# A graph layer's edge tiles cut from 128 edges to 127

## The reference, cut to what matters

```python
def _rgcn_layer(x, W, root, bias, src, dst, seg):
    agg = segment_sum(x[src], seg, num_segments=N_REL * N_NODES)
    agg = agg.reshape(N_REL, N_NODES, -1)
    return einsum('rnd,rde->ne', agg, W) + x @ root + bias
...
h = relu(layer(relu(layer(xn, 0)), 1));  h = sigmoid(layer(h, 2))
x = x + h + mix(xn)          # mix: linear attention over all nodes and a feed-forward part
x = x + moe(layernorm(x))    # 8 experts, the top 2 of each node
```

## Time and profile before

| | |
|---|---|
| median of three runs without the profiler | 8040.71 us (8016.86 to 8065.2) |
| span of the profiled execution, first to last instruction | 6522.0 us |
| median less the span | 1518.7 us |
| busy in the span | PE 83%, POOL 71%, PEld 62%, DVE 31%, ACT 16% |
| phase 0, then the gathers of layers 1, 2 and 3 | 0 to 389, 389 to 2404, 2424 to 4450, 4471 to 6489 us |
| mean granted TensorE clock | 0.920 |

### The profile page before, as it was taken

How to read it: one execution, slowest core, us unless ns; L and a number is a source line. 1 busy time by engine, 2 the same in 40 slices (tenths; PEclk the granted TensorE clock), 3 DMA queues, 4 the chain that set the end, 5 groups by cost and what they waited for, 6 DMA issues and landing times.

```text
span 6522.0 us, 82564 instructions
## 1 busy us (share of the span) xinstructions
PE 5410.7 (83%) x22990; PEld 4060.0 (62%) x22990; DVE 2019.4 (31%) x5385; ACT 1061.6 (16%) x2756; POOL 4625.3 (71%) x4909
## 2 busy tenths in 40 slices
PE   8977777777777778888888888887888888888888
PEld 4445555555555546666666666666777777777776
DVE  3321211122222223332333333333444444444444
ACT  2211111111111111111111111111222222222222
POOL 1057777777777767777777777776777777777776
PEclk9989898889898889999999999999999999999999
DMA  6654444444444444544554444444433333433333
GB/s 195 180 155 137 137 137 137 137 137 137 137 137 137 137 143 144 147 146 146 147 148 146 146 145 146 147 146 149 116 115 115 115 115 115 115 115 115 116 115 93
DMA packets 354380, 887.88 MB, mean 136 GB/s; under 512 B 86234, under 2 KB 179294, under 8 KB 335623
## 3 DMA queue, kind: packets, MB, share of 16 engines
q0 software_dynamic: 232080, 633.91, 33.0%
q10 hardware_dynamic: 114178, 243.16, 12.8%
q1 hardware_dynamic: 7740, 5.99, 0.3%
HBM read 697.11 MB, written 185.60 MB: 135 GB/s over the span
## 4 chain that ended last, share of the span: by engine, by line
POOL 44%; PE 30%; issue 15%; ACTq 5%; DMA 3%; ACT 1%; POOLq 1%; DVE 0%; DVEq 0%; SPq 0%
POOL ring L501 44%; PE ps_out L1403 11%; PE ps_y L1371 8%; PE ps_tr L1570 2%; PE ps_b L1558 2%; DMA ring<-table,gather_idx 2%; PE ps_c L1371 1%; PE ps_b L1371 1%; PE ps_c L1558 1%; ACTq L619 1%; ACTq L740 1%; ACTq L699 1%; ACT y_stage L517 1%; PE ps_y L1656 1%; ACTq L527 1%
## 5 line engine op out<-in xcount | busy, mean ns | idle before, releaser
L501 POOL DMA_INDIRECT ring<-table,gather_idx x4836 | 4580.7, 947 | 1519.4 <-issue 1487.8
L1403 PE MATMUL ps_out<-ring,onehot 128*125 x8400 | 2238.3, 419 | 709.7 <-SPq L428 671.1
L1403 PEld LDWEIGHTS ps_out<-ring,onehot 128*125 128x125 f32 x8400 | 1699.0, 209 | 1131.0 <-issue 857.7
L1371 PE MATMUL ps_y<-W,hT 128*125 128x512 f32 (+1 forms) x2400 | 1016.9, 564 | 0.9 <-ACT hT L564 0.9
L835 DVE COPY y_stage<-ps_y 125x512 f32<-125x512 f32 x150 | 103.7, 692 | 2425.6 <-PE ps_y L1371 2393.6
L1403 PE MATMUL ps_out<-ring,onehot_more 128*125 x2448 | 661.3, 421 | 131.9 <-SPq L428 87.4
L1371 PEld LDWEIGHTS ps_y<-W,hT 128*125 128x125 f32 x2400 | 455.8, 192 | 400.1 <-issue 372.7
L994 DVE TENSOR_TENSOR onehot<-targets,ps_out 128x500 f32<-128x500 f32 x1050 | 646.4, 671 | 172.1 <-issue 117.1
L1403 PEld LDWEIGHTS ps_out<-ring,onehot_more 128*125 128x125 f32 x2448 | 479.5, 205 | 286.8 <-issue 214.7
L517 ACT COPY y_stage<-ps_y 125x512 f32<-125x512 f32 x350 | 204.6, 585 | 1659.1 <-PE ps_y L1371 1653.8
L994 DVE TENSOR_TENSOR onehot_more<-targets,ps_out 128x250 f32<-128x250 f32 x612 | 240.9, 414 | 608.4 <-PE ps_out L1403 490.2
(11 more groups left out here) (193 smaller groups left out, 3208.2 us busy)
## 6 DMA issues: line engine op xcount, KB each, us to landing
table<-y_stage ACTq DMA_DIRECT2D x147, 896.0 KB
ring<-table,gather_idx POOLq DMA_INDIRECT x4836, 2.9
table<-y_stage ACTq DMA_DIRECT2D x147, 104.0 KB
xn_in<-xn_scratch ACTq DMA_DIRECT2D x100, 125.0 KB
base<-y_stage ACTq DMA_DIRECT2D x100, 125.0 KB
base_in<-base ACTq DMA_DIRECT2D x100, 125.0 KB
x_in<-in_x_dram ACTq DMA_DIRECT2D x75, 125.0 KB
xn_scratch<-xn_in ACTq DMA_DIRECT2D x50, 125.0 KB
```

The source lines that it names most:

```text
L501: nc.gpsimd.indirect_dma_start(ring[0:n, c * D:(c + 1) * D], None, table[l], bass.IndirectOffsetOnAxis(ap=gather_idx[0:n, tile:tile + 1].b ...
L1371: last = nc.tensor.matmul(BANK[phase][b][0:WIN, 0:n], hT[parity][:, k, :], W[:, k, b * 2 * D:b * 2 * D + n], start=(k == 0), stop=(k == K ...
L1403: return nc.tensor.matmul(ps_out[w % 2][0:WIN, 0:D], lhsT, ring[:, bass.ds(slot + j * D, D)], start=first, stop=last)
```

## The change

`TILE` becomes 127. A chunk then holds 508 edges. The 206250 edges fill 406 chunks and 2 edges of a 407th, so `FILLED` goes from 403 to 407, while the 408 chunks (`CHUNKS`) of the program's loop stay; POOL skips those past `FILLED`, 5 before and 1 after. Each gather moves 127 rows. In the last chunk the first gather moves 2 rows, and the three behind it, which have no edges, move 127 rows of table row 0. The loads of the edge list are in rows of 508 bytes instead of 512, and the left part of the last block has 88 partitions and 2 edges instead of 75 and 42. One-hots and the multiplies' contraction have 127 partitions. All sizes are fixed when the program is built.

```diff
-TILE = 128
+TILE = 127
...
-        onehot = [sb(f"onehot{i}", [128, TILES, WIN]) for i in range(STATIC)]
-        onehot_more = [sb(f"onehot_more{i}", [128, HALF, WIN]) for i in range(2)]
+        onehot = [sb(f"onehot{i}", [TILE, TILES, WIN]) for i in range(STATIC)]
+        onehot_more = [sb(f"onehot_more{i}", [TILE, HALF, WIN]) for i in range(2)]
...
-        PREP = TB * 128
+        PREP = TB * TILE
...
-                v = dst[:, 0:TB * 128].rearrange("p (b f) -> p b f", f=128)
+                v = dst[:, 0:TB * TILE].rearrange("p (b f) -> p b f", f=TILE)
...
-                            n = min(TILE, edges - tile * TILE)
-                            assert n > 0
+                            left = edges - tile * TILE
+                            n = min(TILE, left) if left > 0 else TILE
+                            assert n > 1
...
-                    nc.vector.tensor_copy((gather_idx, targets)[i % 2][:, b * 128:(b + 1) * 128],
-                                          ps_out[i % 2][:, 0:128]).then_inc(prep_ev, 1)
+                    nc.vector.tensor_copy((gather_idx, targets)[i % 2][0:TILE, b * 128:(b + 1) * 128],
+                                          ps_out[i % 2][0:TILE, 0:128]).then_inc(prep_ev, 1)
...
-                    out, targets[:, bass.ds(col, count)].unsqueeze(2).broadcast_to([128, count, n]),
-                    nodes.unsqueeze(1).broadcast_to([128, count, n]), ALU.is_equal)
+                    out, targets[0:TILE, bass.ds(col, count)].unsqueeze(2).broadcast_to([TILE, count, n]),
+                    nodes[0:TILE, :].unsqueeze(1).broadcast_to([TILE, count, n]), ALU.is_equal)
...
-                    nc.tensor.transpose(ps_out[half][:, 0:128], src[:, b * 128:(b + 1) * 128],
+                    nc.tensor.transpose(ps_out[half][0:TILE, 0:128], src[:, b * TILE:(b + 1) * TILE],
                                         ident[:, :]).then_inc(prep_tr, 1)
...
-                                        ring[:, bass.ds(slot + j * D, D)], start=first, stop=last)
+                                        ring[0:TILE, bass.ds(slot + j * D, D)], start=first, stop=last)
```

More of the change, by code:

```diff
@@ L437, in _ @@
         def _(pool):
-            lo = full_blocks * 128
-            nc.gpsimd.memset(prep_i[:, lo:TB * 128], 0)
-            nc.gpsimd.memset(prep_t[:, lo:TB * 128], 0)
+            lo = full_blocks * TILE
+            nc.gpsimd.memset(prep_i[:, lo:TB * TILE], 0)
+            nc.gpsimd.memset(prep_t[:, lo:TB * TILE], 0)
             nc.gpsimd.memset(order_b[:, ordC - 1:ordC], PADDED)
-            nc.gpsimd.memset(prep_d[:, lo:TB * 128], PADDED).then_inc(prep_zeroed, 1)
+            nc.gpsimd.memset(prep_d[:, lo:TB * TILE], PADDED).then_inc(prep_zeroed, 1)
             nc.gpsimd.memset(ident[:], 1.0).then_inc(consts_made, 1)
```

## The result

The changed kernel takes 14570.42 us (median of 4 runs, 14567.07 to 14572.79), the kernel before 8035.37 us on the same chip (4 runs, 8016.86 to 8065.2). The ratio is 1.8128, with an interval of 1.8087 to 1.8169: slower by 81%, where 0.7% was predicted.

What follows compares the result with a forecast made beforehand. POOL's count of gathers, 1.25 us apart, was taken to set layers 1 and 3, with PE and POOL level in layer 2. Gathers 56 us plus preparation 3 us, added to 8040.7, gave 8100 us (+0.73%), range 8050 to 8165.

Steps and rivals of the forecast that it cites:

- More gathers: In the three layers, 16 more gathers each, 1.25 us apart: 20 + 16 + 20 = 56 us more.
- the units: In layers 1 and 3, 8 us of PE work and 3.3 us of VectorE lie beside POOL's beat, costing nothing.
- preparation: Edge-list loads in rows of 508 bytes for 512: 0 to 12 us more, taken as 3 us.
- The price of one gather: On POOL, a 127-row gather spreads over 16 engines and stays 0.95 us long, so nothing is added.
- one engine, longer generation: Gathers confined to one DMA engine come every 2.2 us, some 12740 us in all; chance 0.05.
- In turn, hidden: Each gather on one DMA engine, in turn, lands 6.7 us later; only layer ends show: 20 us more, 8120; chance 0.05.
- Always the same engine: All gathers on the same DMA engine, 7.1 us each: near 36700 us; chance 0.02.
- faster: With one DMA engine a gather takes 0.65 us and PE sets all layers: 299 us less, near 7745; chance 0.04.
- Span and time: The 1518.7 us between trace span and median time: if fixed, 8100 us (taken); if scaling with the span, 8113 us.

Runs made afterwards that it cites:

- e1_pad128: The changed kernel, but every gather moves 128 rows, the last one unused: 7950.83 us against 7892.93 for the kernel before, ratio 1.0075.

## Why the prediction was wrong, by its own steps

**More gathers, the units, preparation: right.** 4884 gathers, 2544 records, and 59 us were predicted for all of this together; e1_pad128 has it alone: 57.9 us, with 39 to 81 as its interval. The rows of 508 bytes cost nothing that shows, the first gather starts at 385.8 us. The 57.9 us came in a kernel whose layers are not at POOL's beat throughout, so the agreement of the sum does not show the split by layer.

**The price of one gather: this step failed.** It took 127 rows to be spread over 16 engines, eight rows at most on each, and so 0.95 us for the gather; measured are 127 rows on one engine and 2.55 us. The step rests on the 42-row gather, which it held to go by the rounded-up count on the strength of two small packets too many. They are those of the two engines left out: each engine gets as many packets as the busiest, those without data small ones. In the packet records these two have 12 bytes, three pieces of 4 as the others have three rows, and only the 16 last ones have 4. The count fits every size measured: 42 rows, one data packet and one small one on 14 engines, and two small ones on the other 2 (18 small of 32); 126 rows 4 x 16 = 64; 31 rows 9 x 16 = 144; 127 rows 33 x 16 = 528. The other reading, that 14 engines were used since 14 divides 42, was written beside it and put aside by the sentence that engines left out "need no more than the small packet each had", which no row had shown. The rule of the Trainium skill (DMA: Bandwidth & Descriptors, Why a DMA increments its semaphore by 16 and not by 1), that the number of engines is the largest divisor up to 16, fits here at every size tried, and its case of one engine at 127 is the one measured. Its exception with the rounded-up count is stated there for some direct copies; the prediction left that word out and held it to an indirect gather.

**The rival "one engine, longer generation": the right mechanism, too small, and at too small a chance.** It took 8 ns a row from 0.04 us between 3 and 8 rows on an engine, hence 1.9 us and 12740 us. Measured are 13.1 ns and 2.55 us. Two points 0.04 us apart could not give the slope, all the less as the gather of 128 rows lies 0.04 us under the line of the others: with 13 ns the rival would have said 0.95 + 1.56 = 2.5 us. "In turn, hidden" was right that it is not always the same engine (a gather's large packets take 6.5 us together by the packet records, more than the beat of 2.855) and that landing grows, to 8.0 us for its 9.6 (2.9 + 6.7), and wrong that nothing else would. "Always the same engine" and "faster" are refuted by the beat.

**Span and time: wrong too, by 1370 us.** The 1518.7 us between span and median were taken as fixed or in proportion. They lay in a difference between executions: the profiled one of the earlier trace rows was quick, the timed ones have standstills inside the layers. With a longer gather they vanish. Even with the right price, 4884 x 2.855 = 13944 us in place of 6045 would have given 8041 + 7899 = 15940 us, 1370 too many.

## What to carry to other kernels

Choose the row count of an indirect gather by its largest divisor up to 16: 128 keeps 16 engines even and 126 fourteen, while 127, 113 or 31 pay 13 ns of POOL for each row on the one engine (a gather of 31 rows took 1.27 us, one of 128 rows 0.95). Count packets in a window with few gathers and divide by 16: it shows at once how many packets the busiest engine has. Where the profiled execution's time differs from the timed ones by more than the scatter, profile the unchanged kernel again before making a sum on its rows.

## What was not expected of the hardware

- By the packet counts all 16 engines take part in each gather: with 127 rows 496 of 528 packets carry no rows, and the instruction's length follows the longest engine, 13.1 ns a row from 9 rows up, and as long whether a row has 1024 bytes or 256.
- 31, 62 and 124 rows take the same time (1.268, 1.268, 1.292 us).
- With gathers every 1.25 us the engines stand still time and again, up to 29 us at a stretch; POOL's waits are some 1560 us of 8000, and a wait on POOL after each chunk removes them (74 us left) without making the kernel faster. One execution of the same kernel had 32 us of them. The cause is open.
